# Attention loop: the last tile's reciprocal behind the eviction of its place, the scalar key or value eviction behind the head's last exponential

## What is computed

```
z = layernorm(x)
q, k, v = (z @ ((qw - 8) * scale per 128 rows)) for q, k, v
q, k = rope(q), rope(k)                       # x * cos + rotate_half(x) * sin
p = softmax(causal(q k^T / sqrt(128)))        # 4 query heads share one k and v
x = x + (p v) @ ((qw_o - 8) * scale per 128 rows)
```

## Time and profile before

| | us |
|---|---|
| median of 3 runs (lowest, highest) | 2401.65 (2399.18, 2405.0) |
| profiled execution: its own time | 2402.57 |
| profiled execution: span of its trace | 2400.8 |
| busy in the span: TensorE, VectorE, GpSimd, ScalarE | 1953.8, 1420.2, 998.6, 793.9 |
| mean granted TensorE clock (1 is full speed) | 0.815 |

### The profile page before, as it was taken

The page is one execution under the profiler, slowest core; times in us unless marked ns, Lnnn a source line. Parts: engine busy times, 40 slices in busy tenths (PEclk is TensorE's granted clock), DMA queues, the critical chain, the costliest instruction groups (busy, mean ns, idle before and its releaser), DMA issues. The chain is left out here.

```text
span 2400.8 us, 24362 instructions
## 1 busy us (share of the span) xinstructions
PE 1953.8 (81%) x7224; PEld 1183.1 (49%) x7224; DVE 1420.2 (59%) x2176; ACT 793.9 (33%) x1552; POOL 998.6 (42%) x641
## 2 busy tenths in 40 slices
PE   4699999999899999998825789999998526892199
PEld 3366666666666666665525644433333215351144
DVE  6588787778777777886664674333310285405811
ACT  2254544554445455544303401111221313112100
POOL 1254454545444454444310054443850175604630
PEclk9899999999999999999957855555555655996599
DMA  3011011111110111010021000000000100001001
GB/s 128 27 44 44 27 36 44 45 36 36 46 36 27 45 45 42 20 36 27 18 84 70 2 2 0 2 2 2 2 0 19 49 1 1 2 1 79 0 27 44
DMA packets 20619, 71.87 MB, mean 30 GB/s; under 512 B 4596, under 2 KB 5896, under 8 KB 19976
## 3 DMA queue, kind: packets, MB, share of 16 engines
q1 hardware_dynamic: 20488, 70.28, 8.6%
HBM read 61.89 MB, written 8.39 MB: 29 GB/s over the span
## 5 line engine op out<-in xcount | busy, mean ns | idle before, releaser
L602 POOL TENSOR_TENSOR prob<-prob,inv_total 128x512 f32<-128x512 f32 (+3 forms) x256 | 190.0, 746 | 399.8 <-DVE inv_total L537 399.8
L492 DVE SCALAR_TENSOR_TENSOR acc<-pj,sc_o,acc 128x1024 f32<-128x1024 f32 x232 | 293.7, 1278 | 99.3 <-PE pj L623 92.5
L1719 POOL TENSOR_TENSOR dx_w<-dx_w,acc 128x1024 f32<-128x1024 f32 x90 | 225.1, 2501 | 214.8 <-DVE acc L1710 210.5
L492 DVE SCALAR_TENSOR_TENSOR q_acc<-pj,sc_q,q_acc 128x1024 f32<-128x1024 f32 x224 | 286.6, 1279 | 40.2 <-PE pj L623 32.0
L623 PE MATMUL pj<-ctx_hi,w_o 128*128 128x512 f32 x528 | 238.2, 451 | 28.7 <-DVE kv_acc L492 13.5
L623 PE MATMUL pj<-zT_hi,w_q 128*128 128x512 f32 x512 | 225.3, 440 | 2.5 <-DVE q_acc L492 2.1
L623 PE MATMUL pj<-ctx_lo,w_o 128*128 128x512 f32 x528 | 208.0, 394 | 0.0
L676 PE MATMUL ps<-kT,qT 128*128 128x512 f32 (+3 forms) x512 | 187.2, 448 | 25.4 <-issue 13.7
L623 PE MATMUL pj<-zT_lo,w_q 128*128 128x512 f32 x512 | 203.5, 397 | 0.0
L435 ACT ACTIVATE prob<-ps,low_max 128x512 f32<-128x512 f32 (+3 forms) x256 | 134.3, 527 | 163.3 <-DVE low_max L530 146.4
L700 PE MATMUL pv<-probT,v 128*128 128x512 f32 (+3 forms) x512 | 169.6, 433 | 0.0
(11 more groups left out here) (298 smaller groups left out, 3749.3 us busy)
## 6 DMA issues: line engine op xcount, KB each, us to landing
raw_o<-in_w_o SPq DMA_DIRECT2D x33, 512.0 KB, 3.5
raw_q<-in_w_q SPq DMA_DIRECT2D x32, 512.0 KB, 3.6
ln_x<-in_x SPq DMA_DIRECT2D x8, 512.0 KB, 6.5
raw_kv<-in_w_k SPq DMA_DIRECT2D x8, 512.0 KB, 3.5
raw_kv<-in_w_v SPq DMA_DIRECT2D x8, 512.0 KB, 4.5
x<-in_x SPq DMA_DIRECT2D x8, 512.0 KB, 6.9
x_kept<-x SPq DMA_DIRECT2D x1, 4096.0 KB, 11.1
acc<-x_kept SPq DMA_DIRECT2D x1, 4096.0 KB, 12.1
```

Source lines behind the costliest of these rows:

```text
L492: dve.scalar_tensor_tensor(out=dst, in0=pj[slot][:], scalar=scale, in1=dst, op0=ALU.mult, op1=ALU.add).then_inc(evac_v, 1)
L602: pool.tensor_tensor(prob[:, k % PROBS, 0:w], prob[:, k % PROBS, 0:w], inv_total[:, n:n + 1].to_broadcast([P, w]), ALU.mult).then_inc(norm ...
L1719: pool.tensor_tensor(w, w, self.picks[v % 2], ALU.add).then_inc(self.summed, 1)
```

## The change

VectorE's reciprocal of tile 7 moves, within place 10, from before the eviction of that place to behind it. The body of the reciprocal moves into a function `invert`, unchanged. ScalarE's eviction of K0 and V0 is written at place 9 in place of place 8, where it stands behind the exponential of tile 7; it was ahead of it. Nothing is added or removed; TensorE's, GpSimd's and the DMA queue's programs are the same.

```diff
@@ scalar, in emit
-                        if i == 8 and ("K", 0) in units.values():
+                        if i == 9 and ("K", 0) in units.values():
                             scaled_copy(kv_acc, 0, sc_k[:, bass.ds((g + 1) * KT, 1)],
                                         unit_c.at(g, at[j, "K", 0][0] + 1))
-                        if i == 8 and ("V", 0) in units.values():
+                        if i == 9 and ("V", 0) in units.values():
                             due(act, kT_ready, g + 2)
                             scaled_copy(kv_acc, 0, sc_v[:, bass.ds((g + 1) * KT, 1)],
                                         unit_c.at(g, at[j, "V", 0][0] + 1))
@@ vector
+            def invert(g, j, n):
+                k = j * len(TILES) + n
+                due(dve, exp_done, tile_c.at(g, k + 1))
+                due(dve, norm_done, tile_c.at(g, k + 1 - len(TILES)))
+                dve.reciprocal(inv_total[:, n:n + 1], total[:, n:n + 1]).then_inc(inv_done, 1)
+
@@ vector, in emit
-                        if i - 2 in S_PLACE:
-                            n = S_PLACE.index(i - 2)
-                            k = j * len(TILES) + n
-                            due(dve, exp_done, tile_c.at(g, k + 1))
-                            due(dve, norm_done, tile_c.at(g, k + 1 - len(TILES)))
-                            dve.reciprocal(inv_total[:, n:n + 1], total[:, n:n + 1]).then_inc(inv_done, 1)
+                        if i - 2 in S_PLACE[:-1]:
+                            invert(g, j, S_PLACE.index(i - 2))
                         if i in LO_AT:
...
                         if i in units:
...
                                 add_unit(dst, i % 2, sc[:, bass.ds(col, 1)], unit_c.at(g, u + 1),
                                          evac_v_c.at(g, v_n - (KT - len(SPARED)) if kind == "O" else v_n))
+                        if i - 2 == S_PLACE[-1]:
+                            invert(g, j, len(TILES) - 1)
```

## The result

| | before | after |
|---|---|---|
| median, us (lowest, highest) | 2403.32 (2399.18, 2414.36), 4 runs | 2430.63 (2429.97, 2431.4), 4 runs |
| ratio, 95% interval | | 1.0106 [1.0072, 1.0141] |
| span of the profiled execution | 2400.8 | 2429.7 |

What follows compares the result with a forecast made beforehand. The prediction took TensorE's queue, busy 937 of 1000 us, to bound the attention loop. Head 1 at 12.3, head 3 at 2.5 and heads 0 and 2 at 6.4 sum to 21.2 us slower: 2423 us, range 2410 to 2434.

Steps and rivals of the forecast that it cites:

- the forecast's own range: Whole kernel: the range of the main forecast alone, 2419 to 2429 us, given 62 in 100.
- the sum with all upper bounds: Whole kernel: upper ends of 0.6 us in heads 0, 2 and 3 and 1.9 in head 1, together 26 us.
- the clock rival: TensorE's longer wait before O7 in head 1 lowers its clock: 12 us more, 2435 us; 10 in 100.
- The rival in which only the transposes count: Head 1 costs only as much as head 3: 11.4 us slower, 2413 us; 18 in 100.
- The covered case: GpSimd's multiplication ends before TensorE reaches place 12, and the swap has room: not slower, 2401 us; 10 in 100.
- Head 1: Key swap waits for the later qT, so O5's eviction is 1.8 us late (straight 1.7), holding O7: 12.3 us.
- Its start is set by TensorE, not by the reciprocal: VectorE's eviction at place 10 would need to start 0.5 us earlier for the covered case; little spoke for it.
- Heads 0 and 2: Eviction of K0 behind tile 7's exponential makes copy 5 late: 0.52 us in the loop, 0.37 straight, together 6.4.
- priced as hidden beside it: Loop heads 0 and 2: tile 7's transpose, 0.6 us late, meets TensorE 0.5 us late; the pair priced at 0.52.
- Head 3: Tile 7's late transpose delays O0's eviction: 0.45 us a head in the loop, 0.23 straight, together 2.5.
- The next step, unit O0, is as late.: TensorE, behind tile 7's transpose: O0 is late by the same 0.54 to 0.64 us as the transpose.
- Group 7: No eviction at places 8 to 11, so its order is unchanged: 0.

Runs made afterwards that it cites:

- the key buffer: Changed kernel with a separate buffer for the swapped key, so ScalarE's key swap no longer waits for GpSimd's qT: 2425.5 us, 1.0096 to the kernel before.
- The eviction alone: Kernel before with only ScalarE's eviction of K0 and V0 moved to place 9, reciprocal left where it was: 2412.43 us, ratio 1.0035.
- costs 6.1 there by itself: Changed kernel with ScalarE's eviction of K0 and V0 back at place 8, so only the reciprocal is moved: 2426.34 us, 1.0107 to the kernel before.
- Written out: Changed kernel with groups 2 to 5 written out in place of the hardware loop: 2399.16 us, 0.9978 to the kernel before in the same form.
- the remedy alone: Kernel before, groups 2 to 5 written out, with ScalarE's second half swap of the query behind the copy of tile 5: 2374.27 us.
- The kernel before written out: Kernel before with groups 2 to 5 written out in place of the hardware loop: 2382.79 us, 0.9907 to the kernel before.

## Why the prediction was right, and where it was off

**Direction and mechanism: right.** The forecast was 21.2 us slower, 2423 in 2410 to 2434; measured 2430.63, and 26.4 us in the seven groups. That lies above the forecast's own range of 2419 to 2429, and the seven groups lie above the 26 us of the sum with all upper bounds. The result is inside the wide range because that range had been stretched for the clock rival, whose cost before O7 did not come; so the hit is in part luck. The rival in which only the transposes count falls: with the key buffer head 1 loses 6.3 us. The covered case falls: TensorE waits 0.83 us for tile 7 in head 3.1, and every head of groups 0 to 6 but 0.0 becomes longer.

**Head 1:** forecast 12.3, measured 12.0. The steps stand: reciprocal 1.2 us behind the eviction's start, everything on GpSimd moved with it, O5's eviction following the conversion directly, O7 behind it. The loop's part fits (7.2 in both) only because two misses cancel: heads 2.1 and 4.1 cost 1.6 us, heads 3.1 and 5.1 2.0, where K6's eviction starts 0.32 us later by itself. The sentence "Its start is set by TensorE, not by the reciprocal" doesn't hold there: the reciprocal left its place, TensorE's matmuls stood still, and the eviction moved.

**Heads 0 and 2:** forecast 6.4, measured 8.8. Copy 5 came 0.50 us late in head 3.0 (0.5 forecast), and 0.30 in head 1.0 (0.37). Straight: 1.8 against 2.2. Loop: 7.1 against 4.2. The eviction alone costs in the loop what it was priced at (4.0); the reciprocal, priced as hidden beside it, costs 6.1 there by itself.

**Head 3:** forecast 2.5, measured 5.5; 0.9 straight (0.7 forecast), 4.6 in the loop (1.8).

So what was too small is the loop's part, 4.2 + 1.8 forecast and 11.7 measured. The step that failed is "The next step, unit O0, is as late." The transpose of head 2.3 was 0.62 us late, within the 0.54 to 0.64 forecast; but O0, which used to start 0.03 us behind it, then started 0.57 behind it, so it was 1.17 late and its eviction 1.02. I had moved the two as one block. In heads 3.1 and 5.1 the transpose is 0.97 us late, in heads 3.3 and 5.3 0.75, so there the forecast of the transpose was short as well. Head 2.3 before, transpose and O0:

```profile
501.93 0.27 PE L690 MATMUL pt<-ident,prob 128*128 128x128 f32 x1
501.96 0.48 PE L623 MATMUL pj<-ctx_hi,w_o 128*128 128x512 f32 x1
```

Written out, the transpose is 0.29 us late and O0 follows within 0.21 us, and head 3 costs 0.3.

**Group 7:** forecast 0, measured 2.0. Its instructions and their times within the head are the same (to 0.02 us) up to tile 7's transpose at place 12; there the granted clock falls, to 0.68 over the 3.5 us from 1115.5 in head 7.0. The clock rival had the right kind of cost, but the wrong place: not before O7 in head 1. Windows of head 7.0 in the kernel before, then in the changed one (columns as the earlier trace rows); head 7.2 has 1.00 and 0.95 as well:

```profile
1068.50:1100.00 31.50, 27.70 (x124) 18.87 (x123) 22.09 (x32) 15.23 (x32) 14.75 (x13) 1.00 0.10 34
```

```profile
1095.50:1128.00 32.50, 29.08 (x124) 19.98 (x123) 22.12 (x32) 15.22 (x32) 14.75 (x13) 0.95 0.10 33
```

At the loop's turn it also cost more: the 8 us behind it have a clock of 0.65, so 0.35 x 8 = 2.8 us lost, where the same 8 us at 0.79 had lost 1.7. The difference, 1.1 us, is what head 4.0 has over head 2.0 in the table (1.06).

```profile
670.90:678.90 8.00, 7.96 (x23) 5.09 (x24) 2.35 (x3) 2.46 (x5) 0.00 (x0) 0.65 0.01 3
```

## What to carry to other kernels

Before a short step is moved behind a long one on one engine, follow every engine queued behind its result, to the last one: a reciprocal of 0.15 us moved by 1.9 us cost 1.6 us in the heads where a buffer shared between two uses tied another engine's queue to it. Where a wait takes a busy engine's queue dry, add what its next instruction needs to get going (here 0.21 us written out, up to 0.57 in the loop, where 0.03 had been seen), and look whether it sits in a loop. When one late wait is remedied, set the new kernel beside one that has the remedy alone: copy 5 looked like the whole of the eviction's cost until that comparison showed 0.2 us left. And before an order is changed to spare a wait, look in the trace whether that wait exists: here it was 0.4 us in 232 reciprocals.

## What was unexpected in the hardware

**The same instructions ran at two clocks.** Group 7's code is the same in the kernel before and the changed one. Head 7.0 took 31.90 us at a clock of 1.00 in the kernel before and 32.92 at 0.95 in the changed one. The kernel before written out, without the change, has the low clock too (0.95, 32.78 us), and the changed one with the key buffer has not (1.00, 31.93 us). So the change doesn't decide it by itself; both levels, 2.4 and 1.2 GHz, are granted to the same pattern of work in different runs. Windows of head 7.0 in these two kernels:

```profile
1048.00:1080.00 32.00, 28.64 (x123) 19.67 (x122) 21.77 (x32) 15.21 (x32) 14.35 (x13) 0.95 0.11 34
```

```profile
1090.00:1121.50 31.50, 27.66 (x124) 18.87 (x123) 22.11 (x32) 15.22 (x32) 14.75 (x13) 1.00 0.11 34
```

What decides it wasn't tried, and with one trace of each kernel it isn't shown whether it changes from one execution to the next. It is worth about 1 us in each such head, and so 2 of the 28.9 us.

**A hardware loop costs about 1 us in 34 here,** with TensorE busy nearly all the time: written out, the same heads are 0.9 to 1.25 us shorter, and the loop's turn goes with its 2.68 us of idle time. Why a head is slower in the loop is not shown; the waits and addresses that go through registers are the difference in the program. A longer program, with more instructions to fetch, cost nothing that shows.
